# A graph layer's edge softmax, fused into the loop that computes its keys and values

## The reference

```
q = (h @ Wq)                                   # [N, 8 heads, 16]
wk, wv = mlp2(edge_attr_64, ...)               # per-edge weights, 128 wide each
acc_k = sum over s in 0..8 of sh[:, s] * (h[src] @ Cqk[:, s, :])     # sh = edge_attr_9
acc_v = the same with Cv
k, v = acc_k * wk, acc_v * wv
attn = einsum('ehd,ehd->eh', q[dst], k)
amax = segment_max(attn, dst)
ex = exp(attn - amax[dst])
alpha = ex / (segment_sum(ex, dst)[dst] + 1e-16)
upd = segment_sum(v * alpha, dst) @ W_out
out = h @ W_self + upd          # then a normalization over the nodes, and x + it
```

## Time and profile before

| | |
|---|---|
| median of 3 runs | 4183.29 us (4182.96 to 4183.66) |
| the profiled execution | 4178.13 us |
| its span, first to last instruction | 4176.1 us |
| TensorE busy in it | 3459.2 us (83%) |
| VectorE busy | 2924.5 us (70%) |
| GpSimd busy | 2132.7 us (51%) |
| ScalarE busy | 1249.7 us (30%) |
| mean granted TensorE clock | 0.919 |

### The profile page before, as it was taken

One profiled execution on the slowest core, in us unless ns is written; L12 is line 12 of the kernel. 1 busy time (PEld: TensorE's weight loads), 2 busy tenths in 40 slices (PEclk: granted clock), 3 DMA queues, 4 the chain that ended last, 5 costly groups with the idle time before them and its releaser, 6 DMA issues. The chain is left out here.

```text
span 4176.1 us, 91064 instructions
## 1 busy us (share of the span) xinstructions
PE 3459.2 (83%) x26837; PEld 3260.5 (78%) x26837; DVE 2924.5 (70%) x4491; ACT 1249.7 (30%) x2950; POOL 2132.7 (51%) x2231
## 2 busy tenths in 40 slices
PE   2299999999982199999999999999999980577743
PEld 1288888888872099999999999999999970466632
DVE  5266666666650288888888888888888856666632
ACT  1033333333320033333333333333333330233320
POOL 4577777777755455555555555555555530011142
PEclk7699999999995599999999999999999995899975
DMA  6599999999970145544555544555554441488950
GB/s 235 185 281 281 281 279 279 279 279 280 280 224 16 53 125 140 138 136 135 139 140 140 140 135 137 136 140 140 140 138 135 137 111 18 144 263 258 263 147 20
DMA packets 978736, 723.27 MB, mean 173 GB/s; under 512 B 496506, under 2 KB 841931, under 8 KB 978407
## 3 DMA queue, kind: packets, MB, share of 16 engines
q1 hardware_dynamic: 701292, 548.79, 45.0%
q0 software_dynamic: 63840, 89.52, 8.9%
q10 hardware_dynamic: 213558, 84.47, 7.6%
HBM read 390.13 MB, written 333.01 MB: 173 GB/s over the span
## 5 line engine op out<-in xcount | busy, mean ns | idle before, releaser
L1305 ACT ACTIVATE z_hi<-bank 128x512 fp32r<-128x512 f32 (+1 forms) x1010 | 559.4, 595 | 1260.6 <-PE bank L1263 1260.6
L1237 POOL DMA_INDIRECT xg<-h_tab,src_i x808 | 811.1, 1004 | 225.1 <-issue 196.6
L762 POOL DMA_INDIRECT kv<-kv_tab,src_i x808 | 765.8, 948 | 273.7 <-issue 202.6
L1287 PE MATMUL bank<-C_hi,z_hi 128*128 128x256 f32 x4040 | 654.2, 292 | 0.0
L1247 POOL TENSOR_TENSOR kq<-kvs,q_of 128x512 f32<-128x512 f32 x202 | 262.0, 1297 | 675.4 <-DVE kvs L1356 675.4
L1287 PE MATMUL bank<-C_lo,z_hi 128*128 128x256 f32 x4040 | 602.2, 279 | 0.0
L1346 DVE TENSOR_TENSOR z_lo<-bank,z_hi 128x512 fp32r<-128x512 f32 x808 | 519.0, 684 | 118.6 <-ACT z_hi L1305 118.6
L1263 PE MATMUL bank<-ident,z 128*128 128x128 f32 x4040 | 541.7, 273 | 70.1 <-DVE z L1331 62.7
L1331 DVE TENSOR_TENSOR z<-xg,sh 128x1152 f32<-128x1152 f32 x404 | 555.7, 1376 | 9.7 <-DMA xg<-h_tab,src_i 9.7
L1287 PEld LDWEIGHTS bank<-C_lo,z_hi 128*128 128x128 f32 x4040 | 529.1, 188 | 0.0
L1287 PEld LDWEIGHTS bank<-C_hi,z_hi 128*128 128x128 f32 x4040 | 527.9, 189 | 0.0
(11 more groups left out here) (239 smaller groups left out, 4695.8 us busy)
## 6 DMA issues: line engine op xcount, KB each, us to landing
w_tab<-wsb SPq DMA_DIRECT2D x202, 512.0 KB, 3.3
win<-w_tab SPq DMA_DIRECT2D x202, 512.0 KB, 4.9
sum_edge<-rowt ACTq DMA_DIRECT2D x202, 272.0 KB, 3.2
q_edge<-zq SPq DMA_DIRECT2D x202, 256.0 KB
qs<-q_edge SPq DMA_DIRECT2D x202, 256.0 KB, 2.9
v_edge<-kvs SPq DMA_DIRECT2D x202, 256.0 KB, 3.3
vin<-v_edge SPq DMA_DIRECT2D x202, 256.0 KB, 3.2
sum_edge<-rows ACTq DMA_DIRECT2D x202, 136.0 KB
```

Of the source, the lines that this page charges most:

```text
L762: pool.indirect_dma_start(kv[b][:, q, :], None, kv0_tab, bass.IndirectOffsetOnAxis(ap=src_i[:, i * Q + q:i * Q + q + 1], axis=0))\
L1237: pool.indirect_dma_start(xg[b][:, q, :], None, h1_tab, bass.IndirectOffsetOnAxis(ap=src_i[:, i * Q + q:i * Q + q + 1], axis=0))\
L1287: ins = nc.tensor.matmul(bank[6 + q // 2][:, (q % 2) * 2 * O1:(q % 2 + 1) * 2 * O1], zt[b][:, c, e], ct[:, c, :], start=(n == 0), stop=(n ...
L1305: nc.scalar.activation(z_hi[b][f, k, :], bank[ZB[k]][f, :], ACT.Copy).then_inc(hi_out, 1)
```

## The change

The softmax stage and the loop of weighted sums go; their work moves into the tensor-product loop, tile by tile. After the logits of 512 edges (32 columns: 4 tiles times 8 heads) TensorE transposes them (`turn_logits`), two scans of VectorE over 32 partitions and 128 edges, forward and back, give every edge the maximum of its segment inside its tile (`segment_max`; a mask with -BIG where `dst` changes comes from a new table, `mask_tab`, written in the setup stage), TensorE turns it back (`turn_max`), VectorE subtracts (`subtract`), ScalarE takes exp (`weights`), GpSimd weighs v with it (`weigh`), TensorE sums with the one-hot matrix that is there already (`sums`), ScalarE copies sums and maxima (`take_sums`, `copy_max`), and SP stores rows of 144 (128 sums of v, 8 of exp, 8 maxima). Since maxima are now those of a tile, the tail rescales: a scan of maxima over the tiles, exp of differences, and for each node own part and carry, each times exp of its maximum less the larger one. Transposes of `z` use three banks, bank 3 is shared by the spread q, the turned logits and the turned maxima, 4 and 5 take the sums. Most buffers of the loop become four deep.

```
-            ZB = [0, 1, 2, 5, 0]
-            ZB_FREE = [0, -3, -2, -1, 1]
+            ZB = [0, 1, 2, 0, 1]
+            ZB_FREE = [-1, 0, -2, 1, 2]
+            SHARED, SUMS = 3, 4
...
+                    def load_mask(it, i, b):
+
+                        need(sp, seg_ready, i - RING + 1)
+                        sp.dma_start(mask[b][:, :], mask_tab[bass.ds(i * Q, Q), :].unsqueeze(1).broadcast_to([Q, H1, ML]))\
+                          .then_inc(mask_in[b], 16)
+
                     def store(it, i, b):
-                        sp.wait_ge(kv_ready, i * 2 + 2)
-                        sp.dma_start(v1_edge[bass.ds(i, 1)].rearrange("a p (q o) -> p (a q) o", q=Q),
-                                     kvs[b][:, :, O1:2 * O1]).then_inc(v_out[b], 16)
-
-                    pipelined(sp, [(load_sh, 3), (load_drow, 2), (load_q, 2), (store, -1), (load_w, 1)])
...
+                        sp.wait_ge(rows_cp, i * 2 + 2)
+                        sp.dma_start(sum1_edge[bass.ds(i * ST, ST), :].rearrange("(q p) d -> p q d", p=P),
+                                     rows[b][:, :, :]).then_inc(rows_out[b], 16)
+
+                    pipelined(sp, [(load_sh, 3), (load_drow, 2), (load_q, 2), (load_mask, 1), (store, -4), (load_w, 1)], RING)
...
+                    def weigh(it, i, b):
+                        pool.wait_ge(exp_done, i + 1)
+                        pool.tensor_tensor(va[b % 2][:, :, 0:O1].rearrange("p q (h d) -> p q h d", d=DH),
+                                           kvs[b][:, :, O1:2 * O1].rearrange("p q (h d) -> p q h d", d=DH),
+                                           bcast(va[b % 2][:, :, O1:O1 + H1], 3, DH), ALU.mult).then_inc(va_ready, 1)
+
+                    unrolled([(times_q, -1), (weigh, -2), (gather_x, 4)], RING)
...
-                    pipelined(pe, [(t_z(0), 1), (t_z(1), 1), (m_acc(0), 0), (t_z(2), 1), (t_z(3), 1), (m_acc(1), 0),
-                                   (t_z(4), 1), (spread_q, 0), (m_acc(2), 0), (m_acc(3), 0)])
+                    def turn_logits(it, i, b):
+                        pe.wait_ge(attn_ready, i + 1)
+
+                        if isinstance(i, int) and i == NST - 1:
+                            pe.wait_ge(max_copied, i)
+                            pe.wait_ge(below_ready, i)
+                        else:
+                            pe.wait_ge(q_taken, i + 2)
+                        nc.tensor.transpose(bank[SHARED][0:Q * H1, 0:P], attn[b % 2][:, :], ident[:, :]).then_inc(attn_mm, 1)
+
+                    def turn_max(it, i, b):
+                        pe.wait_ge(seg_ready, i + 1)
+                        nc.tensor.transpose(bank[SHARED][:, 0:P], seg_max[:, :], ident[:, :])\
+                                 .then_inc(seg_mm, 1)
+
+                    def sums(it, i, b):
+                        pe.wait_ge(va_ready, i + 1)
+
+                        need(pe, rows_cp, i * 2)
+                        for q in range(Q):
+                            f = slice((q % 2) * (O1 + H1), (q % 2 + 1) * (O1 + H1))
+                            ins = nc.tensor.matmul(bank[SUMS + q // 2][:, f], same[b][:, q, :], va[b % 2][:, q, :],
+                                                   start=True, stop=True)
+                        ins.then_inc(sum_mm, 1)
+
+                    pipelined(pe, [(t_z(0), 1), (t_z(1), 1), (turn_max, -2), (sums, -3), (m_acc(0), 0), (t_z(2), 1),
+                                   (t_z(3), 1), (m_acc(1), 0), (t_z(4), 1), (spread_q, 0), (m_acc(2), 0),
+                                   (turn_logits, -1), (m_acc(3), 0)], RING)
...
+                    pipelined(act, [(hi(0), 1), (hi(1), 1), (copy_max, -2), (weights, -2), (take_sums, -3), (hi(2), 1),
+                                    (hi(3), 1), (hi(4), 1), (take_q, 0)], RING)
...
+                    def segment_max(it, i, b):
+                        dve.wait_ge(attn_mm, i + 1)
+                        dve.wait_ge(mask_in[b], 16 * (it + 1))
+                        dve.tensor_tensor_scan(upto_max[:, :], mask[b][:, 0:P], bank[SHARED][0:Q * H1, 0:P], -BIG,
+                                               ALU.add, ALU.max).then_inc(upto_ready, 1)
+                        dve.wait_ge(upto_ready, i + 1)
+
+                        need(dve, seg_mm, i)
+                        rev = slice(None, None, -1)
+                        dve.tensor_tensor_scan(seg_max[0:Q * H1, rev], mask[b][:, 1:P + 1][:, rev], upto_max[:, rev], -BIG,
+                                               ALU.add, ALU.max).then_inc(seg_ready, 1)
...
+                        dve.tensor_tensor(below[b % 2][:, :], attn[b % 2][:, :], bank[SHARED][:, 0:Q * H1], ALU.subtract)\
+                           .then_inc(below_ready, 1)
...
-                    pipelined(dve, [(product(1), -1), (lo(0), 1), (lo(1), 1), (outer(0), 2), (lo(2), 1), (lo(3), 1),
-                                    (outer(1), 2), (lo(4), 1), (logits, -1), (build, 1), (product(0), 0)])
-
+                    pipelined(dve, [(product(1), -1), (lo(0), 1), (lo(1), 1), (subtract, -2), (outer(0), 2), (lo(2), 1),
+                                    (lo(3), 1), (logits, -1), (outer(1), 2), (lo(4), 1), (build, 1),
+                                    (segment_max, -1), (product(0), 0)], RING)
```

The stages of lines 1380 to 1628 are deleted. In the tail `carry_over` is replaced by a max scan, an exp of differences, four small matmuls that spread the factors over the heads' columns, and two scans with them; after the gathers the two parts get their factors:

```
+                    step(dve.tensor_tensor_scan(full[0:H1, MX, :], broken[:, :], last[0:H1, MX, :], -BIG, ALU.add, ALU.max))
...
+                    step(dve.tensor_tensor_scan(full[0:H1, EX, :], scale[:, 1, :], last[0:H1, EX, :], 0.0, ALU.mult, ALU.add))
...
+                    step(dve.tensor_tensor_scan(full[:, V, :], keep[:, :], last[:, V, :], 0.0, ALU.mult, ALU.add))
...
+                    for k, t in enumerate((own, car)):
+                        step(dve.tensor_tensor(t[:, :, 0:O1].rearrange("p j (h d) -> p j h d", d=DH),
+                                               t[:, :, 0:O1].rearrange("p j (h d) -> p j h d", d=DH),
+                                               bcast(ratio[:, k, :, :], 3, DH), ALU.mult))
+                    step(dve.tensor_tensor(own[:, :, 0:O1], own[:, :, 0:O1], car[:, :, 0:O1], ALU.add))
```

More of the change, by code:

```diff
@@ L965, in feature_parts @@
         def feature_parts(F):
-            return [(a, min(a + P, F)) for a in range(0, F, P)]
+            bounds = (0, O1, O1 + H1, F2) if F == F2 else (0, F)
+            return list(zip(bounds, bounds[1:]))
         def transpose_last_rows(pe, lrows, F, got, done):
@@ L1175, in gnn @@
             wsb = [sb(f"win{b}", [P, Q, 2 * O1], F32, ph) for b in range(2)]
-            kvs = [sb(f"kvs{b}", [P, Q, 2 * O1], F32, ph) for b in range(2)]
+            kvs = [sb(f"kvs{b}", [P, Q, 2 * O1], F32, ph) for b in range(RING)]
             kq = sb("kq", [P, Q * O1], F32, ph)
@@ L1631, in gnn @@
-        ph = ExitStack()
-        with ph:
-            lrows = sb("lrows7", [P, 7, F1], F32, ph)
-            last = sb("last7", [O1, 2, NTR], F32, ph)
-            full = sb("full7", [O1, 2, NTR], F32, ph)
-            cshift = sb("cshift7", [O1, 2, NTR], F32, ph)
-            crows = sb("crows7", [P, 7, F1], F32, ph)
-            own = sb("own7", [NP, NJ, F1], F32, ph)
-            car = sb("car7", [NP, NJ, F1], F32, ph)
+            lrows = sb("lrows7", [P, 7, F2], F32, ph)
+            last = sb("last7", [O1, 3, NTR], F32, ph)
@@ L1640, in gnn @@
+            own = sb("own7", [NP, NJ, F2], F32, ph)
+            car = sb("car7", [NP, NJ, F2], F32, ph)
             updT = sb("updT", [O1, NJ * NP], F32, ph)
@@ L1682, in _ @@
                 def _(pe):
-                    transpose_last_rows(pe, lrows, F1, last_got, last_mm)
+                    transpose_last_rows(pe, lrows, F2, last_got, last_mm)
+                    pe.wait_ge(scale_ready, 1)
+                    pe.wait_ge(last_out, 6)
+                    for k in range(2):
+                        for n, (a, b) in enumerate(halves):
+                            ins = nc.tensor.matmul(bank[2 * k + n][:, 0:b - a], heads[:, :], scale[:, k, a:b],
+                                                   start=True, stop=True)
+                        ins.then_inc(heads_mm, 1)
                     pe.wait_ge(shift_ready, 1)
@@ L1743, in _ @@
-                    step(dve.reciprocal(car[:, :, O1:F1], own[:, :, O1:F1]))
-                    for h in range(H1):
-                        step(dve.tensor_tensor(own[:, :, h * DH:(h + 1) * DH], own[:, :, h * DH:(h + 1) * DH],
-                                               car[:, :, O1 + h:O1 + h + 1].broadcast_to([NP, NJ, DH]), ALU.mult))
+                    step(dve.tensor_tensor(ratio[:, 1, :, :], car[:, :, O1 + H1:F2], bcast(over[:, :], 2, H1), ALU.mult))
+                    step(dve.tensor_tensor(ratio[:, 1, :, :], ratio[:, 1, :, :], bcast(absent[:, :], 2, H1), ALU.add))
@@ new lines, in _ @@
+                    step(dve.tensor_tensor(top[:, :, :], own[:, :, O1 + H1:F2], ratio[:, 1, :, :], ALU.max))
+                    step(dve.tensor_tensor(ratio[:, 0, :, :], own[:, :, O1 + H1:F2], top[:, :, :], ALU.subtract))
```

(11 more changed lines are left out.)

403 lines of the change are left out of this document (138 added, 265 removed).

## The result

The changed kernel takes 3826.6 us (median of 4 runs, 3825.4 to 3829.4) against 4183.1 for the kernel before (4 runs beside it, 4179.7 to 4183.7): a ratio of 0.915, 95% interval 0.9134 to 0.9166. That is 356.6 us less; the forecast was 331.4 less, 3851.9 us, in a range of 3822 to 3945. The profiled execution took 3826.9 us with a span of 3825.1.

The account below looks back on a forecast made before the run. TensorE was taken to pace the loop. From the median 4183.3 us: 596.3 removed, 250.5 added in the loop, 9.7 drain, 1.7 setup, 3.0 tail, net -331.4, gives 3851.9 us, range 3822 to 3945.

Parts of the forecast that it names:

- What paces the loop: Fused loop: TensorE alone paces it, its added instructions paid in full; period 10.87 us, 250.5 us added; chance 0.73.
- The price of `sums`: Four 128x136 products on TensorE in each fused-loop iteration: 1.02 us, lower end 0.92.
- the transposes: `turn_max` and `turn_logits` on TensorE in each iteration: 0.11 us each, 0.22 in all.
- The drain: End of the fused loop, the chain after its last `logits`: 9.7 us added once, between 8 and 13.
- Setup: Setup stage, ending with two stores of masks: 1.7 us added once, 0 to 3.
- Tail: VectorE work after `car_got`: 17.1 us instead of 14.1, plus 3.0 (1 to 5).
- the cover: Tail: `own` gathers hide the longer carry chain, 15 to 18 us later; 4 us left, nothing charged.
- The base: Starting time for the difference: the runs' median, 4183.3 us, with the profiled execution 5.2 under it.
- The timetable: One iteration laid out by engine: VectorE 9.5 of 10.87 us, GpSimd 8.0, a late scan having 0.9 of slack.
- `weigh`: GpSimd product in the fused loop: 1.30 us, allowed up to 2.6, which would hold back nothing.
- The VectorE rival: VectorE sets the loop's pace if two scans cost over 1.8 us together; 3933 us at 2.2, 4034 at 2.7; chance 0.14.
- The GpSimd rival: GpSimd sets the loop's pace if `weigh` takes over 4.2 us; 4050 us at 5.2; chance 0.07.

Follow-up runs that it names:

- run 1: The changed kernel with the four matmuls of `sums` issued twice in each iteration: 4012.4 us, ratio 0.9592 to the kernel before.
- run 2: The changed kernel with the weights and weighed v held as float32r, so `sums` runs in that form: 3736.8 us, ratio 0.893 to the kernel before.
- Run 11: The changed kernel with both `sums` and `spread_q` in float32r, `weigh` staying on GpSimd: 3636.1 us, ratio 0.87 to the kernel before.
- run 12: The changed kernel with both `sums` and `spread_q` in float32r and `weigh` moved to VectorE: 3633.9 us, ratio 0.8691 to the kernel before.
- run 4: The changed kernel with `outer(0)` put ahead of `subtract` on VectorE: 3851.1 us, ratio 0.9208 to the kernel before.
- Run 7: The changed kernel with two extra copies of `weigh` behind it on GpSimd: 4033.5 us, ratio 0.965 to the kernel before.
- run 10: The changed kernel with two GpSimd memsets behind `weigh`, in place of two extra copies of it: 3829.5 us, ratio 0.9161 to the kernel before.
- run 9: The changed kernel with one extra copy of `weigh` behind it on GpSimd: 3828.1 us, ratio 0.9159 to the kernel before.

## Why the prediction was right, and where it was off

**What paces the loop**: right. TensorE is busy for all 1300 us at clock 1.00, and runs 1, 2, 11 and 12 move the time by what they put on or take off TensorE: 185.9 us for 186, 89.8 for 97, 190.5 and 192.7 for 187. The time landed in the range, but only 4.6 us above its lower end; the misses below nearly all point the same way.

**The price of `sums`**: the largest miss. The prediction took 1.02 from the start of one group of matmuls to the next in the old loop and named 0.92 as the lower end. It is 0.92, by the fused trace and by doubling it. With 0.11 each for the transposes, as forecast, the period grew by 1.15 instead of 1.24: 18 us over 202 iterations. The old loop shows the same price when its loads are read:
```profile
3962.50 0.99 PEld L1601 LDWEIGHTS bank<-va,samf 128*128 128x128 f32 x8 [0.57 <-issue]
...
3963.42 0.47 PEld L1591 LDWEIGHTS bank<-ident,dcolf 128*128 128x128 f32 x4
```
They are 0.92 apart, as in all 192 groups of its window. After the idle spell of 0.33 the first matmul starts 0.01 behind its load, the next group's first one 0.11 behind, so start to start reads 0.10 too much.

**The drain**: 9.7 forecast, 8.7 measured, and two errors hide in that. The chain behind the last `logits` takes 10.2 us, 0.5 more than forecast (the last `sums`, at the lower clock, 2.18 for 1.3), and the 1.55 that the old loop took there was not taken off. That they nearly cancel is luck. **Setup**: 1.7 forecast (its terms add up to 1.9); the loop starts 1.1 later. **Tail**: 3.0 forecast, 3.2 measured. VectorE took 17.0 us after the last `car` gather's landing, against 14.1 (forecast 17.1). The `own` gathers took 42.3 us instead of 39.5: five took 1.4 to 2.6 us instead of 1.2 while VectorE's longer carry chain ran, two before. A `car` gather that took 3.6 us before did not recur. These two, neither of them forecast, nearly cancel, so that 3.2 stands so near 3.0 is in part luck. The last carry rows were issued by 3697.7, the first `car` gather began at 3706.5: the cover held, with nearly 9 us less the landing; the forecast had left 4 behind the landing. **The base**: the prediction took its difference from the median; 5.6 of the 25 us are the profiled runs' distance from theirs (18 are `sums`, 1.0 the drain, 0.6 the setup, less 0.2 of tail).

**The timetable**: right in its order and near in its times. Counted from `t_z(0)`: `turn_max` 0.9, `sums` 1.0 to 1.9, `outer(0)` to 4.2 (4.4 forecast), VectorE idle 0.73 before `lo(2)` (0.8). `seg_max` has 1.2 us of slack (0.9). VectorE works 9.26 us a round (9.5). GpSimd works 7.07; the 8.0 forecast counts the time of issue too, and with its 1.05 it is 8.1. The two agree because `weigh` took 0.34 more than forecast and the old queue was put too high: the earlier trace rows give 6.4 with its idle time of issue, not 6.65.

**`weigh`** took 1.64, between the forecast 1.30 and its bound of 2.6, for a reason that is neither: alone it takes 1.06, less than the plain product's 1.28, and the rest is `outer(0)`. The Trainium skill, "SBUF — State Buffer", section "Who interferes with whom", has a VectorE instruction with two SBUF inputs and a GpSimd reader exclude each other. The trace agrees: 2511.28, where `outer(0)` ends, plus 1.06 is 2512.34, and `weigh` ended at 2512.19, 0.15 sooner than if all of it had waited.

**The VectorE rival**: its threshold of 1.8 us for the scans was set a little low; 1.97 still costs nothing. Longer scans were not run, but run 4 shows the rival's way of costing time: `seg_max` 1.3 us later is more than the slack of 1.2, and TensorE waits.

**The GpSimd rival**: its threshold was wrong, and this is the step that failed in kind. The prediction let GpSimd cost nothing until its queue was longer than the period, 4.2 us for `weigh`. The changed kernel never came near it, so the time did not suffer. Run 7 puts 3.8 there and loses 207 us; run 10 fills the queue to the brim and loses nothing. The prediction had weighed the exclusion only in one direction, VectorE holding up `weigh`, and that direction is free. In the other, a late product with `weigh` ready behind it keeps `outer(0)` out for as long as GpSimd goes on. The 2.6 us that it called harmless are (run 9, 2.7 us), but the next copy isn't. What keeps the changed kernel safe is room in two places: the 1.5 us that GpSimd waits ahead of its product (185.2 us in 121 rounds), and another 1.1 from the product's end (2509.42) to that of the `Exp` which makes `weigh` ready (2510.51). Run 11 has next to nothing of the first left and 0.6 to 0.8 of the second, and loses nothing. The prediction's timetable held both, and it never asked what would happen without them.
